# Routed layers that add their gated results to the tokens' rows in memory

## The reference

```
layer 2: routing_weights = softmax(x @ gate_w.T)         # 8 experts, inner width 352
         topk_w, topk_i  = top_k(routing_weights, 2);  topk_w /= sum(topk_w)
         for e in 8: w_e = sum(where(topk_i == e, topk_w, 0))
                     out += w_e[:, None] * ((silu(x @ w_gate[e]) * (x @ w_up[e])) @ w_down[e])
layer 3: shared_out = sum over 2 experts of gelu(x @ Wsh_up) @ Wsh_down      # inner width 256
         top_v, top_i = top_k(softmax(x @ W_router), 2)   # 16 experts, not renormalised
         routed_out = sum over chosen e of top_v * (gelu(x @ Wrt_up[e]) @ Wrt_down[e])
```

## Time and profile before

| | |
|---|---|
| profiled execution | 3416.8 us, its span 3415.1 us |
| median of 3 runs | 3413.54 us |
| TensorE busy | 2536.0 us, 74% |
| VectorE busy | 2322.0 us, 68% |
| ScalarE busy | 1604.3 us, 47% |
| GpSimd busy | 1131.4 us, 33% |
| mean granted TensorE clock | 0.873 of full speed |
| memory read, written | 210.34 MB, 93.32 MB |

### The profile page before, as it was taken

How to read it: one execution, slowest core, us unless ns; L and a number is a source line. 1 busy time by engine, 2 the same in 40 slices (tenths; PEclk the granted TensorE clock), 3 DMA queues, 4 the chain that set the end, 5 groups by cost and what they waited for, 6 DMA issues and landing times. The chain is left out here.

```text
span 3415.1 us, 42603 instructions
## 1 busy us (share of the span) xinstructions
PE 2536.0 (74%) x14172; PEld 1217.5 (36%) x14172; DVE 2322.0 (68%) x3741; ACT 1604.3 (47%) x2262; POOL 1131.4 (33%) x815
## 2 busy tenths in 40 slices
PE   2987897799679735766673899809788888668990
PEld 1532333344234311222222677605322222324660
DVE  6665763465857788899886566565688885555664
ACT  2544553244232665455541556505466675224870
POOL 5755763020001115666660222055510000002434
PEclk9988999799779857898895899959799999779995
DMA  3650321111000000000001777545502201104995
GB/s 130 199 174 13 93 63 75 46 38 37 0 4 11 1 0 1 0 0 0 0 0 52 256 248 234 166 121 199 187 11 75 63 14 63 50 25 146 317 306 166
DMA packets 162831, 305.94 MB, mean 90 GB/s; under 512 B 33299, under 2 KB 80671, under 8 KB 160246
## 3 DMA queue, kind: packets, MB, share of 16 engines
q1 hardware_dynamic: 139462, 223.49, 18.9%
q0 software_dynamic: 23216, 80.49, 8.3%
HBM read 210.34 MB, written 93.32 MB: 89 GB/s over the span
## 5 line engine op out<-in xcount | busy, mean ns | idle before, releaser
L2100 DVE TENSOR_REDUCE ac_nmax<-ac_M 128x1 f32<-128x512 f32 (+1 forms) x768 | 497.2, 687 | 152.0 <-PE ac_M L1914 147.2
L2078 ACT ACTIVATE ac_PT<-ac_S 128x1024 f32<-128x1024 f32 x384 | 371.2, 1018 | 160.0 <-PE ac_S L1949 137.1
L2924 POOL TENSOR_TENSOR sc_hc<-sc_h,sc_cs 128x1024 f32<-128x1024 f32 x128 | 300.6, 2354 | 170.3 <-DVE sc_h L3038 113.1
L3038 DVE TENSOR_TENSOR_SCAN sc_h<-sc_dA,sc_dB 128x1024 f32<-128x1024 f32 x128 | 292.1, 2283 | 7.0 <-ACT sc_dA L3004 7.0
L2959 PE MATMUL sc_y<-sc_hc,ident 128*128 128x512 f32 x512 | 254.1, 626 | 2.3 <-POOL sc_hc L2924 2.3
L3004 ACT ACTIVATE sc_dA<-ss_delta,sc_A 128x511 f32<-128x511 f32 x256 | 166.0, 682 | 30.8 <-DVE sc_h L3038 30.3
L3030 DVE TENSOR_TENSOR sc_dB<-ss_du,sc_b 128x1024 f32<-128x1024 f32 x128 | 156.2, 1220 | 27.8 <-PE sc_b L2937 17.2
L2937 PE MATMUL sc_b<-ss_bc,sc_sel 128*128 128x512 f16 x128 | 54.7, 428 | 159.9 <-DVE sc_dB L3030 126.6
L3009 ACT ACTIVATE sc_cs<-sc_c 128x512 f32<-128x512 f32 x128 | 76.2, 596 | 203.2 <-POOL sc_hc L2924 160.3
L1914 PE MATMUL ac_M<-KT,QT 64*128 64x512 f16 (+1 forms) x384 | 141.5, 431 | 39.8 <-DVE ac_nmax L2100 23.0
L1001 DVE SCALAR_TENSOR_TENSOR mo_up16l<-mo_up,mo_up16h 128x1408 f16<-128x1408 f32 (+1 forms) x80 | 117.1, 1465 | 72.0 <-ACT mo_up16h L945 71.8
(11 more groups left out here) (495 smaller groups left out, 6195.8 us busy)
## 6 DMA issues: line engine op xcount, KB each, us to landing
slot_results<-mo_o SPq DMA_DIRECT2D x56, 512.0 KB
mo_up<-in_w_gate SPq DMA_DIRECT2D x24, 704.0 KB, 5.6
mo_up<-in_w_up SPq DMA_DIRECT2D x24, 704.0 KB, 7.0
keys_t<-ap_kto SPq DMA_DIRECT2D x32, 512.0 KB, 2.7
queries_t<-ap_qto SPq DMA_DIRECT2D x32, 512.0 KB, 2.7
mo_up<-in_exp_up SPq DMA_DIRECT2D x32, 512.0 KB
mo_dn<-in_exp_down SPq DMA_DIRECT2D x32, 512.0 KB
mo_dn<-in_w_down SPq DMA_DIRECT2D x24, 512.0 KB
```

What stands on the lines that cost most here:

```text
L2078: nc.scalar.activation(PT[:, n % PTB, :, :], psS[:, 2 * (n % 2):2 * (n % 2) + 2, :], ACT.Exp, scale=SCALE / (SQK * SQK)).then_inc(exp_done, 1)
L2100: last = v.tensor_reduce(out[:, :, 0], sc[:, 0:MAIN], AX.X, ALU.max)
L2924: nc.gpsimd.tensor_tensor(hc[:, m % RC, :, :], h[:, m % RH, :, :], cs[:, m % 2, :].unsqueeze(1).to_broadcast([P, W, S]), ALU.mult).then_in ...
L3038: nc.vector.tensor_tensor_scan(h[:, m % RH, :, :].rearrange("p c s -> p (c s)"), dA[:, m % 2, :, :].rearrange("p c s -> p (c s)"), dB[:, m ...
```

## The change

The routed block starts by copying x into memory: `sums2` in layer 2, the output tensor itself in layer 3. After that each step scales its results by the gates of its slots while ScalarE copies them out of PSUM, and GpSimd adds the rows to those of their tokens with two indirect transfers that accumulate. A step's transfers are issued only after those of the step before have landed, since a token has rows in two steps. Slots with no token add to 256 spare rows behind the 2048. The `fetch` part, `slot_results`, and `store_block` go. Layer 2 loads x back in eight transfers and computes `bn_stats` from it.

The router computes for every slot the row (`step_row`) and the gate (`step_gate`), the latter by 32 more matmuls of twice the columns, in a high and a low half. The number of steps is (4096 + n_exp x 255) // 256, 23 and 31. Gathers are issued two steps ahead.

```diff
-        NS = 2 * T // SLOTS + n_exp
+        NS = (2 * T + n_exp * (SLOTS - 1)) // SLOTS
 # router_block, VectorE
-            nc.vector.tensor_tensor(h4, h4, tokenf[:].unsqueeze(2).to_broadcast([P, NT, 4 * NS]), ALU.mult
-                                    ).then_inc(placed, 1)
+            nc.vector.tensor_tensor(hot_t[:].rearrange("p (t j) h -> p t (j h)", j=2),
+                                    hot_h[:].rearrange("p (t j) h -> p t (j h)", j=2),
+                                    tokenf[:].unsqueeze(2).to_broadcast([P, NT, 4 * NS]), ALU.mult).then_inc(placed, 1)
+            for i, part in enumerate((top_h, top_l)):
+                last = nc.vector.tensor_tensor(hot_g[:, :, i, :], hot_h[:], spread(part[:], 2 * NS), ALU.mult)
+            last.then_inc(gates_placed, 1)
 # routed_block, SP
-                if not first:
-                    store(s - 1, 1 - w)
             load(0, 0, False)
             load(1, 1, False)
+            sp.dma_start(sums[0:T, :].rearrange("(t p) d -> p t d", p=P), env.x[:]).then_inc(x_out[0], 16)
+            sp.dma_start(sums[T:T + SLOTS, :].rearrange("(t p) d -> p t d", p=P), env.x[:, 0:HS, :]).then_inc(x_out[1], 16)
             run_steps(sp, step)
+            if not final:
+                for w in range(2):
+                    sp.wait_ge(added[w], 16 * HS * ((NS + 1 - w) // 2))
+                for i in range(NX):
+                    sp.dma_start(env.x[:, i * XT:(i + 1) * XT, :],
+                                 sums[i * XT * P:(i + 1) * XT * P, :].rearrange("(t p) d -> p t d", p=P)).then_inc(x_back[i], 16)
 # routed_block, GpSimd
+            def add_rows(s, w, first):
+                nc.gpsimd.tensor_copy(cur_row[:, w, :], step_row[:, bass.ds(s * HS, HS)]).then_inc(row_done, 1)
+                pool.wait_ge(row_done, s + 1)
+                if first:
+                    pool.wait_ge(x_out[0], 16)
+                    pool.wait_ge(x_out[1], 16)
+                else:
+                    pool.wait_ge(added[1 - w], 8 * HS * turns(s - 1, 1 - w))
+                pool.wait_ge(o_done, HS * (s + 1))
+                for h in range(HS):
+                    pool.indirect_dma_start(sums, bass.IndirectOffsetOnAxis(cur_row[:, w, h:h + 1], 0), o32[:, w, h, :], None,
+                                            compute_op=ALU.add).then_inc(added[w], 16)
             def step(s, w, first, early, last):
-                if not last:
-                    gather(s + 1, 1 - w, not first)
+                if not (isinstance(s, int) and s + 2 >= NS):
+                    gather(s + 2, w, True)
+                if not first:
+                    add_rows(s - 1, 1 - w, isinstance(s, int) and s == 1)
 # routed_block, ScalarE
             def results(s, w):
-                act.wait_ge(stored[w], 8 * turns(s, w))
+                if not (isinstance(s, int) and s < 2):
+                    act.wait_ge(added[w], 8 * HS * (turns(s, w) - 2))
+                nc.scalar.activation(cur_gate[:, w, :], step_gate[:, bass.ds(s * HS, HS)], ACT.Copy).then_inc(gate_done, 1)
+                act.wait_ge(gate_done, s + 1)
                 for h in range(HS):
                     act.wait_ge(dn_done, HS * s + h + 1)
-                    nc.scalar.activation(o32[:, w, h, :], po[h][:], ACT.Copy).then_inc(o_done, 1)
+                    nc.scalar.activation(o32[:, w, h, :], po[h][:], ACT.Copy, scale=cur_gate[:, w, h:h + 1]).then_inc(o_done, 1)
 # routed_block, VectorE: the loop of 8 turns over fetched results goes; layer 2 alone has
+                for t in range(NT):
+                    dve.wait_ge(x_back[t // XT], 16)
+                    nc.vector.bn_stats(out=env.stats[:, t, :], in_=env.x[:, t, :])
```

More of the change, by code:

```diff
@@ L343, in _ @@
             for n in range(2 * NT):
-                last = nc.tensor.matmul(p_token[:], hot_p[:, n, :], hot_h[:, n, :], start=(n == 0), stop=(n == 2 * NT - 1))
+                last = nc.tensor.matmul(p_token[:], hot_p[:, n, :], hot_t[:, n, :], start=(n == 0), stop=(n == 2 * NT - 1))
             last.then_inc(inverted, 1)
+            pe.wait_ge(gates_placed, 1)
+            for n in range(2 * NT):
+                last = nc.tensor.matmul(p_gate[:], hot_p[:, n, :], hot_g[:, n, :, :], start=(n == 0),
+                                        stop=(n == 2 * NT - 1))
+            last.then_inc(gates_inverted, 1)
         @block.vector
@@ L748, in routed_block @@
     passes = [(0, 0), (1, 0), (0, 1)]
-    CT = HS
+    XT = 2
+    NX = NT // XT
     with ExitStack() as ctx:
@@ L872, in _ @@
-            for v in range(2):
-                fetch(0, v, False)
-            with pool.Fori(1, NT // (2 * CT)) as i:
-                for v in range(2):
-                    fetch(i, v, True)
+            add_rows(NS - 1, (NS - 1) % 2, False)
+            for w in range(2):
+                pool.wait_ge(added[w], 16 * HS * ((NS + 1 - w) // 2))
         @block.tensor
@@ L929, in _ @@
             run_steps(pe, step)
-            down(NS - 1, 1, False)
+            down(NS - 1, (NS - 1) % 2, False)
         @block.scalar
@@ L989, in _ @@
             run_steps(act, step)
-            results(NS - 1, 1)
+            results(NS - 1, (NS - 1) % 2)
         @block.vector
@@ L1088, in layer_ffn @@
         coef = keep("coef", [P, NT, max(shared, 1)], F32)
-        routing = (keep("gates", [P, NT, 2], F32), keep("slot", [P, NT, 2], I32), keep("step_expert", [P, NS], I32),
-                   keep("step_token", [P, 2 * NS], I32))
-        slots_out = nc.dram_tensor(f"slot_results{index}", (NS * SLOTS, D), F32, kind="Internal").ap()
+        routing = (keep("step_expert", [P, NS], I32), keep("step_token", [P, 2 * NS], I32), keep("step_row", [P, 2 * NS], I32),
+                   keep("step_gate", [P, 2 * NS], F32))
+        final = index == 3
+        sums = env.out if final else nc.dram_tensor(f"sums{index}", (T + SLOTS, D), F32, kind="Internal").ap()
         router = ins["gate_w_t"] if index == 2 else ins["W_router"]
@@ L3080, in layer_xattn2 @@
     env.ssm.close()
-def store_block(nc, env, out):
-    with ExitStack() as ctx:
-        stored = env.sem("out_stored")
-        block = ctx.enter_context(nc.Block())
-        @block.sync
-        def _(sp):
-            sp.dma_start(out.rearrange("(t p) d -> p t d", p=P), env.x[:]).then_inc(stored, 16)
-            sp.wait_ge(stored, 16)
 LAYERS = ("xattn0", "ffn0", "xattn1", "ffn1", "xattn2", "ffn2", "xattn3", "ffn3")
@@ L3100, in build_program @@
         env = Env(nc, stack, ins)
-        env.count = 0
+        env.count, env.out = 0, out
         nc.disable_value_cache = True
@@ L3108, in build_program @@
             env.recycle()
-        store_block(nc, env, out)
 def laid_out(v):
@@ L3166 @@
         ins[name] = nc.dram_tensor(f"in_{name}", a.shape, mybir.dt.from_np(a.dtype), kind="ExternalInput").ap()
-    out = nc.dram_tensor("out_x", (T, D), F32, kind="ExternalOutput").ap()
+    out = nc.dram_tensor("out_x", (T + SLOTS, D), F32, kind="ExternalOutput").ap()
     build_program(nc, ins, out)
     r = run_bass_kernel_spmd(nc, [arrays], core_ids=[0])
-    return r.results[0]["out_x"].reshape(B, S, D)
+    return r.results[0]["out_x"][0:T].reshape(B, S, D)
```

116 lines of the change are left out of this document (46 added, 70 removed).

## The result

The changed kernel takes 3478.34 us, the median of 4 runs (3473.16 to 3482.23), against 3411.12 us for the kernel before beside it: a ratio of 1.0196, interval 1.0174 to 1.0219. It is slower, by about 2%. The forecast was 3387 us, and 3478 lies outside its range of 3330 to 3470.

What follows compares the result with a forecast made beforehand. TensorE was taken to set layer 2's step, and transfers layer 3's, with TensorE close behind. 3416.8 + 11 + 15 - 13.4 + 6 - 39.5 - 64 + 58.3 = 3390.2, less 3.3: 3387 us; range 3330 to 3470.

Steps and rivals of the forecast that it cites:

- 1 routers: Router blocks of both layers: two one-hot products by gates and small instructions, 4.9 and 5.9 us, sum +11.
- 2 x stored first: Start of both routed stages: storing x on SP's queue delays the third load of weights, +15 us, between 0 and 29.
- 3, 4 layer 2's steps: Layer 2's routed stage: one step fewer, -13.4 us, and slip of 0.25 us in each remaining step, +6.
- 5 tail of layer 2: After layer 2's last copy: fetches go, x is reloaded, 27 us in all instead of 66.5, -39.5.
- 5 tail of layer 3: After layer 3's last copy: fetches and the last plain store go, 12.5 us instead of 76.4, -64.
- term 4: Layer 2's remaining steps: GpSimd's 9.17 us of waiting cover 3 to 4 us more work; +6 (0 to +23).
- Term 6: Layer 3's steps: T is the longest of transfers, GpSimd's work and a ring; T = 8.9 us, +58.3.
- The ring: Layer 3: result, its additions, gathers behind them, transposes two steps later; 16.5 to 18.0 us, T = 8.2 to 9.0.
- the clock: Rival in layer 3: TensorE's granted clock falls now and then, adding 0.9 us to the mean step; kept inside the range.
- the longer issue: Rival in layer 3: an addition's issue costs 0.97 us more, T = 9.4 to 9.9, at 9.9 3418 us; chance 0.17.
- The slower rival: Layer 3: additions wait for the previous pair's landing A, T = A + 1.8; 3446 us at A = 9; chance 0.32.
- The forecast's own sign: Layer 2's step growing by over 1 us means term 4 is wrong and an accumulating transfer costs more than two gathers.

Runs made afterwards that it cites:

- e1: The changed kernel with the gathers for step s+3 issued ahead of the additions of step s-1 on GpSimd; 3415.9 us, ratio 1.0017.
- e10: The changed kernel with twelve unused filler matmuls on TensorE before the wait for gathered rows in each layer 3 step; 3458.7 us, ratio 1.0134.
- e2: The changed kernel with plain indirect writes in place of the accumulating ones, so sums are left out of the output; 3411.6 us, ratio 0.9999.
- e3: The changed kernel with additions of even and odd steps going to two memories, so no pair waits for the one just before; 3478.9 us, ratio 1.0194.
- e5: e1 and e3 together: gathers ahead, additions of even and odd steps to two memories; 3383.2 us, ratio 0.9916.
- e6: e1 with GpSimd's program written out step by step, without the two index copies of each step; 3402.8 us, ratio 0.9971.
- e8: New way in layer 2 only (gathers ahead, x stored behind third load, gates' copy in a ScalarE wait), layer 3 as in e7; 3358.0 us, ratio 0.9836.
- e7: The kernel before with only the step counts cut, to 23 and 31 from 24 and 32; 3389.1 us, ratio 0.9926.
- e9: The changed kernel, both layers: gathers ahead, x stored behind third load, no index copies, gates' copy in a ScalarE wait; 3405.1 us, ratio 0.9982.
- e11: e1 with plain indirect writes in place of the accumulating ones, so sums are left out of the output; 3356.6 us, ratio 0.9830.

## Why the prediction was wrong

Against the profiled span (3415.1 to 3478.8, +63.7) its terms came out so. The rows are the first and last copies and what ends each tail:

```profile
1925.29 1.26 ACT L996 ACTIVATE mo_o<-mo_po,mo_cur_gate 128x512 f32<-128x512 f32 x2
2248.14 0.69 ACT L996 ACTIVATE mo_o<-mo_po,mo_cur_gate 128x512 f32<-128x512 f32 x1 [1.26 <-PE mo_po L935]
2260.42 4.00 SPq L852 DMA_DIRECT2D x_res<-sums  x8
2277.20 1.80 POOL L1178 MEMSET stk<- 128x2048 f16 x1 [20.19 <-POOLq L72]
3141.46 1.26 ACT L996 ACTIVATE mo_o<-mo_po,mo_cur_gate 128x512 f32<-128x512 f32 x2
3459.88 1.26 ACT L996 ACTIVATE mo_o<-mo_po,mo_cur_gate 128x512 f32<-128x512 f32 x2
3469.70 1.54 POOL L882 DMA_INDIRECT out_x<-mo_o,mo_cur_row  x1 [0.30 <-issue]
```

| term | forecast | measured |
|---|---|---|
| 1 routers | +11 | +9.4 |
| 2 x stored first | +15 | +10.0 |
| 3, 4 layer 2's steps | -7.4 | +27.1 |
| 5 tail of layer 2 | -39.5 | -38.1 |
| 5 tail of layer 3 | -64 | -58.7 |
| 6 layer 3's steps | +58.3 | +118.2 |
| between the layers | 0 | -4.3 |

The first two are read where the gathered rows are first used: 4.8 and 4.6 us later for the routers, and from there to the first copy 3.7 and 6.3 us more. The steps run from first to last copy: 295.8 to 322.9 and 200.8 to 319.0 us. The tails end at the next block (66.5 to 28.4) and at the end of the span (76.4 to 17.7). The -4.3 us stand in layer 3's attention, which the change doesn't touch; they are not explained. Terms 1, 2 and 5 were right to within 6 us each. Two failed. Of the +27.1 in layer 2, one step less is -12.9, as forecast; the other 22 steps cost +40 where term 4 had +6 and a bound of +23. In layer 3, 30 intervals at 10.6 us and not 8.9 make 52 of the 60 us that the term was short by; most of the rest is that the sum took the steady 6.8 us for every step of the kernel before, whose mean over the stage is 6.48.

**Term 6 had the right mechanism and the wrong size.** The ring was forecast at about 17.3 us with a middle landing and is 21.5. Its legs, forecast and measured, from the chain above: from the transposes to the copies' end 6.9 and 8.8 us (plus 0.5 forecast for the gates' copy), because after a wait TensorE starts at half speed (the eight transposes take 1.96 us in that row and 1.04 in the earlier trace rows; with the first products that follow this makes the 1.9 us); until GpSimd acts, 0.24 and 0.8; two additions and a copy, 3.75 and 4.9 (3299.11 to 3304.03), of which 0.8 is that an issue with a sum takes 1.6 us and not the 1.2 of a gather; first to second gather, 1.52 and 1.33; landing behind the additions, 4.35 (from transfers in the quiet tail) and 5.6. That makes +4.2 us a ring, 2.1 a step. e1 shows that it is the order (62 us over both layers), e10 that the clock is in it (20 us), e2 that the sums are in it (67 us over both layers, with the order kept). These overlap and don't add up. The forecast had the longer issue and the clock as rivals, each alone, and the clock inside the range at 0.9 us; it did not see that they are legs of one ring and come together.

**Term 4 failed in its reasoning.** "3 to 4 us more work on GpSimd, whose 9.17 us of waiting cover it" took idle time for room. GpSimd's wait was now for the result, and the gather stood behind it. The timeline of layer 2, one ring:

```profile
2078.93 1.62 POOL L882 DMA_INDIRECT sums<-mo_o,mo_cur_row  x1 [9.47 <-ACT mo_o L996]
...
2084.80 1.90 POOL L865 DMA_INDIRECT mo_g<-normalised,mo_cur  x1 [0.30 <-issue]
...
2109.65 1.62 POOL L882 DMA_INDIRECT sums<-mo_o,mo_cur_row  x1 [9.47 <-ACT mo_o L996]
```

```profile
2092.93 1.97 PE L905 MATMUL mo_yT<-ident,mo_g 128*128 128x128 f32 x8 [3.74 <-DMA mo_g<-normalised,mo_cur]
```

GpSimd still idles 9.47 us, and TensorE still waits 3.74 us for rows that landed 8.13 us after their issue. The next additions of the same ring are issued at 2109.65, so the ring is 30.7 us for two steps, 15.4 each. The forecast drew this ring for layer 3 alone. Two rows of the kernel before, the transposes and the copies of one step of layer 2:

```profile
2062.47 1.04 PE L886 MATMUL mo_yT<-ident,mo_g 128*128 128x128 f32 x8
```

```profile
2077.27 1.06 ACT L972 ACTIVATE mo_o<-mo_po 128x512 f32<-128x512 f32 x2
```

These are 15.9 us, and with the other legs of the forecast (0.5 for the gates, 0.24, 3.75, 1.52, 4.35) the ring would have been 26.3 us, 13.1 a step against the step's 13.4. So there was next to no cover: 0.5 us more on the legs of a ring uses it up. The leg that brought it is mostly the landing of the gathers behind the additions, 8.1 us against 4.35, though the DMA engines are far from full in this stage (0.75). e1 takes 1.36 us off each of layer 2's steps. The forecast's own sign, a layer 2 step longer by over 1 us, came; but the cause that it tied to it, the price of the transfer, is only part: e1 keeps the transfers, and the middle step falls from 15.4 us to 14.0.

**The slower rival named the right sign and the wrong cause.** "Additions queue behind each other" had 3446 to 3498 us, where the time lies, but e3 takes that wait away and nothing moves; that its times hold the measured one is luck. It is the second limit, behind the ring (e5, e6, and e10, where it sets the step). The DMA engines' price, 2.9 us a pair in the changed kernel and 3.35 in e1, lies between the ends given, 1.94 and 3.88. It did not set the changed kernel's step, at a DMA share of 0.76; whether it is close behind in e5 and e6, at 0.92, no run here separates.

## What to carry to other kernels

When work that waits for a result is put on an in-order engine ahead of work that feeds the pipeline, draw the whole ring in every stage, not only in the tight one, and count idle time on that engine as cover only for what it does not hold up. Put the feeding transfer ahead of the draining one where its buffer is free by then: here that was worth 62 us with the same transfers. Where a stage is bound by transfers, as layer 3 was, accumulating ones can cost more than the tail that they save, while the compute-bound layer 2 gains: e8, with the new way in layer 2 alone, is 31 us under e7, and e9, with it in both layers (and no index copies), 47 us above e8.

## What the hardware showed beyond what was expected

- An indirect transfer that accumulates costs 0.6 us more of GpSimd for its issue (1.61 against 1.01) and about three times a plain one's share of the DMA engines (3.35 against 1.15 us a pair in e1 and e11, 2.9 against 0.95 in the changed kernel and e2; estimates, with 1.94 us taken off for the gathers).
- In layer 3 of e6 the next pair of additions, which waits for the landing of the one before, goes out 6 to 9 us behind that one's second issue. In the quiet tail of layer 2 the reload of x could start 5.0 us behind it (2255.45 to 2260.42).
- Work added to an idle TensorE made the kernel 20 us faster: the granted clock went from 0.84 to 1.00, and TensorE no longer began at half speed behind its waits (e10).
- SP's queue is held behind a large store: the 4.19 MB store of x was issued in 0.43 us at 1889.32, but the small one right behind it, at 1889.79, took 13.3 us to issue, and the third load left at 1904.16 instead of 1893.79.
